# One stage of a recurrent kernel re-ordered: VectorE's loop begins with the new hidden state, a TensorE product moves to step 3, and the forget gate is made in columns

## The reference, cut to what matters

```python
x = x + attention_over_two_keys(x, cond)          # layer 0
x = x + shared_and_routed_experts(x, cond)        # layer 1: 1 shared, 8 routed, top 2
x = x + linear(x) + f(cond)                       # layer 2
# layer 3, a gated recurrence over the 1024 tokens, h starts as cond, c as 0
def step(carry, xz_t):
    prev_h, prev_c = carry
    z = xz_t + prev_h @ Wh                        # [2, 1024], xz = x @ Wx + b
    ai, af, ao, ag = jnp.split(z, 4, axis=1)
    next_c = sigmoid(af) * prev_c + sigmoid(ai) * tanh(ag)
    next_h = sigmoid(ao) * tanh(next_c)
x = x + hs
```

## Time and profile before

| | us |
|---|---|
| median of 3 runs | 2004.42 |
| the profiled execution's own time | 2006.19 |
| its span, first to last instruction | 2004.4 |
| PE busy | 1848.3 |
| PEld busy | 1462.6 |
| DVE busy | 1351.8 |
| POOL busy | 1134.2 |
| ACT busy | 812.2 |

### The profile page before, as it was taken

How to read it: one execution, slowest core, us unless ns; L and a number is a source line. 1 busy time by engine, 2 the same in 40 slices (tenths; PEclk the granted TensorE clock), 3 DMA queues, 4 the chain that set the end, 5 groups by cost and what they waited for, 6 DMA issues and landing times. The chain is left out here.

```text
span 2004.4 us, 255266 instructions
## 1 busy us (share of the span) xinstructions
PE 1848.3 (92%) x113164; PEld 1462.6 (73%) x113164; DVE 1351.8 (67%) x7215; ACT 812.2 (41%) x4757; POOL 1134.2 (57%) x4950
## 2 busy tenths in 40 slices
PE   7899999999999999999999999999999999999998
PEld 5677777777777777777777777777777777777776
DVE  2566666666666666666666666666666666676666
ACT  2344444444444444444444444444444444444443
POOL 3555555555555555555555555555555555555555
PEclk9899999999999999999999999999999999999999
DMA  4000000000000000000000000000000000000000
GB/s 166 3 4 3 3 4 3 3 3 4 3 3 4 3 3 3 4 3 3 4 3 3 4 3 3 3 4 3 3 4 3 3 3 4 3 3 4 3 3 3
DMA packets 57724, 14.67 MB, mean 7 GB/s; under 512 B 56176, under 2 KB 56304, under 8 KB 57200
## 3 DMA queue, kind: packets, MB, share of 16 engines
q1 hardware_dynamic: 57712, 14.50, 3.1%
HBM read 12.37 MB, written 2.10 MB: 7 GB/s over the span
## 5 line engine op out<-in xcount | busy, mean ns | idle before, releaser
L916 PEld LDWEIGHTS psum<-wh_sb,h_ring 128*2 128x2 f32 (+1 forms) x32768 | 519.6, 90 | 446.0 <-DVE h_ring L740 414.9
L916 PE MATMUL psum<-wh_sb,h_ring 128*2 128x64 f32 (+1 forms) x32768 | 690.8, 219 | 138.7 <-DVE h_ring L740 121.4
L926 PE MATMUL psum<-h_ring,wh_sb 128*32 128x2 f32 x65536 | 768.7, 173 | 3.5 <-issue 3.5
L926 PEld LDWEIGHTS psum<-h_ring,wh_sb 128*32 128x32 f32 x65536 | 725.0, 109 | 13.3 <-issue 3.7
L517 ACT ACTIVATE f_act<-psum 128x4 f32<-128x4 f32 x1024 | 177.2, 173 | 763.7 <-DVE psum L711 755.1
L711 DVE STREAM_TRANSPOSE psum<-psum 128x64 f32<-128x64 f32 x1024 | 264.6, 258 | 306.6 <-PE psum L916 306.4
L789 PE MATMUL psum<-up_sb,x 128*32 128x512 f32 x2064 | 282.7, 605 | 0.0
L713 DVE STREAM_TRANSPOSE psum<-psum 128x64 f32<-128x64 f32 x1024 | 270.6, 264 | 16.1 <-PE psum L916 3.0
L795 PE MATMUL psum<-down_e,hid_t 128*16 128x256 f32 x3096 | 268.0, 381 | 0.6 <-ACT down_e L498 0.6
L723 DVE TENSOR_TENSOR_SCAN psum<-addend,psum 128x16 f32<-128x16 f32 x1024 | 199.2, 195 | 71.4 <-ACT psum L520 29.3
L740 DVE SCALAR_TENSOR_TENSOR h_ring<-o_act,psum 128x4 f32<-128x4 f32 x1024 | 163.0, 159 | 116.8 <-ACT psum L526 87.7
(11 more groups left out here) (141 smaller groups left out, 2224.7 us busy)
## 6 DMA issues: line engine op xcount, KB each, us to landing
x_a<-in_x SPq DMA_DIRECT2D x129, 16.0 KB, 1.6
x_s<-in_x SPq DMA_DIRECT2D x129, 16.0 KB, 1.7
up_sb<-in_up SPq DMA_DIRECT2D x1, 2048.0 KB, 12.6
out_y<-y_sb SPq DMA_DIRECT2D x128, 16.0 KB, 1.4
down_sb<-in_down SPq DMA_DIRECT2D x1, 1536.0 KB, 8.2
wx_sb<-in_wx SPq DMA_DIRECT2D x1, 1024.0 KB, 14.7
wh_sb<-in_wh SPq DMA_DIRECT2D x1, 1024.0 KB, 17.9
wkv_sb<-in_wkv SPq DMA_DIRECT2D x1, 512.0 KB, 4.2
```

The lines of the kernel that those rows point to most:

```text
L916: last = nc.tensor.matmul(z[32 * j:32 * j + row + B, :], h_ring[:, prev, c, WIN - B - row:WIN], wh_v[:, c, g, j, :], start=False, stop=(c ...
L926: last = nc.tensor.matmul(by_row(z)[32 * j:32 * (j + 1), m, row:row + B], wh_v[:, c, g, j, 32 * m:32 * (m + 1)], h_ring[:, prev, c, WIN - ...
```

## The change

- `recur_row` takes one half c of the contraction, `recur_column` one half m of the gate. Only the input gate is left in rows. The order of a step is: input gate c = 0 (8 matmul instructions), forget gate m = 0 in columns (16), input gate c = 1 (8), forget gate m = 1 (16), candidate (32), output gate (32).
- The transpose of `z_f` (L711) and its semaphore are gone; ScalarE reads `z_f` itself. `base_f` is a transpose and stands between L720 and the scan of step 7.
- The copy under the input gate goes from VectorE's step 0 to ScalarE's step 7, between its tanh of input gate and candidate and that of the output gate; it waits for `f_based`.
- VectorE's loop is turned: writing h is the head of the next step (`close`), so step 7's h is written after the branch back. The first h comes from the same instruction with prepared operands; the last is written after the loop.
- The transpose of `hid_s` goes from the end of step 7 to its head. `stream_mm` goes from step 0 to the end of step 3, behind `attend`, and `x3_made` is signalled behind it.

```diff
             def base_f(up_to):
-                nc.vector.tensor_copy(z_f, z_x[:, GF, :]).then_inc(f_based, up_to)
+                nc.vector.transpose(z_f, z_x[:, GF, :]).then_inc(f_based, up_to)
...
-                    act.wait_ge(f_turned, now)
+                    act.wait_ge(f_made, now)
                     nc.scalar.activation(f_act[:, :].rearrange("p (c b) -> p c b", b=B),
-                                         by_row(t_f)[:, :, step], ACT.Tanh).then_inc(a_f, 1)
+                                         by_row(z_f)[:, :, step], ACT.Tanh).then_inc(a_f, 1)
...
+                    if u == 7:
+
+                        act.wait_ge(f_based, act.snap(t + (u + 1 + U)))
+                        nc.scalar.activation(z_i, z_x[:, GI, :], ACT.Copy).then_inc(i_based, U)
                     act.wait_ge(o_made, now)
...
             with dve.Fori(READY, READY + T, U) as t:
+                now = t
                 for u in range(U):
+                    dve.wait_ge(cell_tanh, now)
+                    if u == 1:
+
+                        dve.wait_ge(h_read, now)
+                    close((u - 1) % U)
                     now = dve.snap(t + (u + 1))
                     if u == 0:
 
-                        nc.vector.tensor_copy(z_i, z_x[:, GI, :]).then_inc(i_based, U)
                         nc.vector.transpose(z_c, z_x[:, GC, :])
                         nc.vector.transpose(z_o, z_x[:, GO, :]).then_inc(x_turned, U)
...
-                    dve.wait_ge(f_made, now)
-                    nc.vector.transpose(t_f, z_f).then_inc(f_turned, 1)
                     dve.wait_ge(i_made, now)
                     nc.vector.transpose(t_i, z_i).then_inc(i_and_c_in, 1)
-                    if u == 7:
-                        dve.wait_ge(f_turned, now)
-                        dve.wait_ge(x_injected, now)
-                        base_f(U)
 
                     dve.wait_ge(a_f, now)
                     nc.vector.scalar_tensor_tensor(out=keep_out, in0=f_act[:, :], scalar=1.0, in1=cell_c,
                                                    op0=ALU.add, op1=ALU.mult).then_inc(terms_in, 1)
+                    if u == 7:
+                        dve.wait_ge(x_injected, now)
+                        base_f(U)
...
-                    recur_row(z_f, GF, u * B, prev).then_inc(f_made, 1)
-                    if u == 0:
                         pe.wait_ge(i_based, now)
-                    recur_row(z_i, GI, u * B, prev).then_inc(i_made, 1)
+
+                    recur_row(z_i, GI, u * B, prev, 0)
+                    recur_column(z_f, GF, u * B, prev, 0)
+                    recur_row(z_i, GI, u * B, prev, 1).then_inc(i_made, 1)
+                    recur_column(z_f, GF, u * B, prev, 1).then_inc(f_made, 1)
                     if u == 0:
                         pe.wait_ge(x_turned, now)
-                    recur_column(z_c, GC, u * B, prev).then_inc(i_and_c_in, 1)
-                    recur_column(z_o, GO, u * B, prev).then_inc(o_made, 1)
+                    recur_columns(z_c, GC, u * B, prev).then_inc(i_and_c_in, 1)
+                    recur_columns(z_o, GO, u * B, prev).then_inc(o_made, 1)
                     if u == 0:
 
                         pe.wait_ge(hid_st, now)
-                        stream_mm(x1)
                         down_mm(0).then_inc(stream_made, U)
...
-                        attend(attn_b, w1_own[:, :]).then_inc(x3_made, U)
+                        attend(attn_b, w1_own[:, :])
+                        stream_mm(x1).then_inc(x3_made, U)
```

More of the change, by code:

```diff
@@ L291, in cond_stack_kernel @@
         o_made = sem("o_made")
-        f_turned = sem("f_turned")
         i_and_c_in = sem("i_and_c_in")
@@ L350, in _ @@
             pool.sem_inc(y_stored, 16)
-            for s in (f_made, i_made, o_made, f_turned, a_f, cell, cell_tanh, hid, x_turned, i_based):
+            for s in (f_made, i_made, o_made, a_f, cell, cell_tanh, hid, x_turned):
                 pool.sem_inc(s, READY)
@@ L682, in _, with close @@
             base_f(READY + U)
-            dve.wait_ge(terms_set, 3)
+            nc.vector.tensor_copy(z_i, z_x[:, GI, :]).then_inc(i_based, READY + U)
+            dve.wait_ge(terms_set, 5)
+            def close(slot):
+                nc.vector.scalar_tensor_tensor(out=h_ring[:, slot, :, WIN - B:WIN],
+                                               in0=o_act[:, :].rearrange("p (c b) -> p c b", b=B), scalar=1.0,
+                                               in1=c_tanh.rearrange("p (c b) -> p c b", b=B),
+                                               op0=ALU.add, op1=ALU.mult).then_inc(hid, 1)
             with dve.Fori(READY, READY + T, U) as t:
+                now = t
                 for u in range(U):
+                    dve.wait_ge(cell_tanh, now)
+                    if u == 1:
+                        dve.wait_ge(h_read, now)
+                    close((u - 1) % U)
                     now = dve.snap(t + (u + 1))
                     if u == 0:
-                        nc.vector.tensor_copy(z_i, z_x[:, GI, :]).then_inc(i_based, U)
                         nc.vector.transpose(z_c, z_x[:, GC, :])
@@ L709, in _ @@
                         invert_inv(now)
-                    dve.wait_ge(f_made, now)
-                    nc.vector.transpose(t_f, z_f).then_inc(f_turned, 1)
+                        dve.wait_ge(hid_s_out, now)
+                        turn(0, hid_s[:, :], hid_st, U)
                     dve.wait_ge(i_made, now)
                     nc.vector.transpose(t_i, z_i).then_inc(i_and_c_in, 1)
-                    if u == 7:
-                        dve.wait_ge(f_turned, now)
-                        dve.wait_ge(x_injected, now)
-                        base_f(U)
                     dve.wait_ge(a_f, now)
@@ L732, in _ @@
                         hidden_a(now)
[L733 to L736, removed]
-                    if u == 0:
[L739 to L743, removed]
+            dve.wait_ge(cell_tanh, READY + T)
+            close(U - 1)
         @block.tensor
@@ L910, in _, with recur_row, recur_column, recur_columns @@
             attend(attn_b, w1_own[:, :])
+            stream_mm(x1)
             pe.wait_ge(wh_scaled, 2)
-            def recur_row(z, g, row, prev):
+            def recur_row(z, g, row, prev, c):
+                for j in range(J):
+                    last = nc.tensor.matmul(z[32 * j:32 * j + row + B, :],
+                                            h_ring[:, prev, c, WIN - B - row:WIN], wh_v[:, c, g, j, :],
+                                            start=False, stop=(c == C - 1), skip_group_check=True)
+                return last
+            def recur_column(z, g, row, prev, m):
                 for c in range(C):
                     for j in range(J):
-                        last = nc.tensor.matmul(z[32 * j:32 * j + row + B, :],
-                                                h_ring[:, prev, c, WIN - B - row:WIN], wh_v[:, c, g, j, :],
+                        last = nc.tensor.matmul(by_row(z)[32 * j:32 * (j + 1), m, row:row + B],
+                                                wh_v[:, c, g, j, 32 * m:32 * (m + 1)],
+                                                h_ring[:, prev, c, WIN - B:WIN],
                                                 start=False, stop=(c == C - 1), skip_group_check=True)
                 return last
-            def recur_column(z, g, row, prev):
+            def recur_columns(z, g, row, prev):
                 for m in range(C):
[L924 to L929, removed]
+                    last = recur_column(z, g, row, prev, m)
                 return last
```

10 lines of the change are left out of this document (5 added, 5 removed).

## The result

| | before | after |
|---|---|---|
| median, us | 2004.66 | 4034.95 |
| lowest to highest | 2003.37 to 2005.9 | 4034.54 to 4036.44 |
| span of the profiled execution | 2004.4 | 4032.7 |
| granted TensorE clock | 0.997 | 0.649 |
| a batch of 8 steps, from h to h | 15.23 | 31.20 |

The account below looks back on a forecast made before the run. It took a step-by-step chain through the input gate as the bound, with candidate and TensorE close behind. Terms -0.25 - 0.11 + 0.14 + 0.04 + 0.13 = -0.05 us a batch, x 128 = -6.4, gave 1998.0 us, range 1970 to 2034.

Parts of the forecast that it names:

- TensorE's order, every step: Swapping 16 row instructions for 32 columns delays what follows by 0.035 us a step, between minus 0.04 and +0.07.
- step 0: Batch's first step: input base copied earlier, branch back hidden behind step 7's scan; 2.07 to 1.82 us, 0.25 saved.
- step 1: Second step: without step 0's layer 2 product its rows are not late; 1.93 to 1.82 us, 0.11 saved.
- product in step 3, `hid_s` turned first: Layer 2 product fits step 3, `hid_s` transpose fits step 7's head: no cost, at worst 0.07 and 0.05 us.
- columns in steps 0 to 6: Forget gate's columns cost 0.035 us in each step where TensorE bounds, 0.01 in the others.
- step 7 beyond e1's, its columns included: Base transpose and ScalarE's copy delay step 7 by 0.13 us (0.05 to 0.23), besides the columns' cost there.
- What the missing transpose gives: nothing: Dropping the forget gate's transpose saves nothing: input path was last by only 0.02 us, and the candidate gets later.
- The pace of 8.2 ns: Time per added column early in a step: 32 take 0.26 us; the dearer case was 9.1 ns, 0.29 us.
- the slack of 0.025 us: Candidate ready before L520 needs it, so the 0.035 us delay costs only 0.01 in steps TensorE does not bound.
- Rival 1: Columns run at the mean pace, 9.1 ns: +0.23 us a batch, +29 us, 2034 us; chance 0.25.
- Rival 2: Forget columns fill the rows' waits: -0.65 us a batch, 1921 us, or half of it, 1963; chance 0.15.
- rival 3: Going from columns to rows drains TensorE, 0.17 us in each of 8 steps: 2172 us; chance 0.05.

Follow-up runs that it names:

- e11: The whole changed kernel plus one argument, a hint for TensorE's branch back; 2272.49 us.
- e1: The changed kernel with the forget gate back in rows with its transpose, the rest of the change kept; 1961.39 us, ratio 0.978 to the kernel before.
- e16: e11 with the layer 2 product (`stream_mm`) back at the start of step 0's piece; 2096.28 us, ratio 1.049 to the kernel before.
- e2: The changed kernel, forget columns kept, with half of the output gate's contraction left out; 2237.83 us, ratio 1.116 to the kernel before.
- e9: e2 with the input gate's rows together and all forget columns after them; 2299.13 us in the median.
- e10: e2 with the layer 2 product (`stream_mm`) back at the start of step 0's piece; 2097.72 us.
- e4: The kernel before with eight tiny overwritten matmuls added in step 4, 1808 instructions, no hint; 2797.8 us.

## Why the prediction was wrong

The step that failed is *TensorE's order, every step*. It priced 16 rows against 32 columns as time on TensorE and never as length of its program. As work, the 256 instructions more in an iteration cost some tenths of a microsecond, in the table below; through the fetches, and the lower clock that comes with them, they cost 13.9 us a batch (31.20 less 17.30 of e11), x 128 = 1780 us. No rival had it, and the range could not hold it. The row to look at was on the page before: the instruction queue's 9 packets, with the instruction count beside it.

Taken apart, in us a batch, from 15.23 to 31.20:

| part | forecast | measured | from |
|---|---|---|---|
| step 0 | -0.25 | -0.24 | e1 |
| step 1 | -0.11 | -0.11 | e1 |
| product in step 3, `hid_s` turned first | 0 | 0 | e1 |
| columns in steps 0 to 6 | +0.145 | +0.37 | quiet batches of e11 and e16 against e1 |
| step 7 beyond e1's, its columns included | +0.165 | +0.19 | same |
| falls of the clock, nothing fetched | none | +1.87 | e11's mean less its quiet batch |
| fetches | none | +13.90 | after less e11 |

- Steps 0 and 1 are right to 0.01 us, and the branch back hides behind the scan as argued.
- "What the missing transpose gives: nothing" holds; the candidate became what L520's successor waits for, as forecast.
- The columns are mis-sized twice. The pace of 8.2 ns gave +0.035 us; by the traces the 32nd candidate column of a step 4 begins 0.84 us after h in e2 and e11 and 0.78 in e1 (medians over quiet batches), 0.055 later. And the slack of 0.025 us is not there: L518 of e11, which waits for these columns, begins 0.27 us after the 32nd of them, and L520 of e1 began 0.28 after it, so the candidate was there less than 0.01 us before it was needed. All steps paid 0.05 to 0.06.
- That slack was read in a step 0, taken as one where the candidate comes last. But its row names L713 as the releaser; and 127 of the 129 waits for L713, which the prediction took for the chain of every step, are waits of step 0.
- Rival 1's whole sum was +0.23 a batch, 2034 us; e11's quiet batch of 15.43 is +0.21, and not by luck: for columns and step 7 together it had 0.59 and 0.56 was measured. Without fetches and falls that rival would have been the result.
- Step 7 had the right mechanism and was 0.02 too small. The copy took 0.21 us and held up its follower for 0.12, as estimated.
- Rival 2 (hidden columns) is refuted by e2, whose steps got longer, and rival 3 (a drain of 0.17 us a step) by e2 and e9.
- The clock has no term in the prediction. The kernel before and e1 are at 1.0 in every batch but the first ones; e3, which is e1 with half of the output gate left out, has falls in 18 of 126. That moving one product spares most of e2's falls is shown (e10); what keeps the kernel before free of them is not.

## What to carry to other kernels

Before adding instructions to an engine's loop, count the loop: read the instruction queue's packets on the page, and compare the iteration's length with the room. Here TensorE kept 2033 instructions but not 2065 with a hint on the branch back, and 1792 but not 1808 without. A form that trades streaming time for more, shorter matmuls can lose there even where its arithmetic is right, and "idle <- issue" together with instruction packets in proportion to the iterations is how it shows. Test the parts of a change one by one: the half that was only meant as a rearrangement gave 2.2%, and 2.8% once the pieces were spread.

## What the hardware did that I had not expected

- A block of 16 KB of instructions costs some 3.7 us when a loop is fetched again, one block after the other; 16 more instructions took a kernel from 2038 to 2798 us.
- Eight tiny matmuls in one column group cost 0.51 us (e4's step 5, 2.40 against 1.89), some 32 ns for each of their 16 matmul instructions; columns spread over four groups come 8 to 9 ns apart. The eight also write the same output, and which of the two matters wasn't tested:

```profile
1005.61 0.19 PE L971 MATMUL psum<-wh_sb 128*32 128x2 f32 x1
1005.66 0.58 PE L971 MATMUL psum<-wh_sb 128*32 128x2 f32 x14
1006.10 0.17 PE L971 MATMUL psum<-wh_sb 128*32 128x2 f32 x1
```

- With TensorE in flight over 90% of the time by the page, the granted clock can still fall in nearly every batch (e2, 93% busy, 0.82), and moving one product of four matmul instructions (0.62 us from first start to last end) by three steps brought most of it back (e10).
